# Long convolution with a gated feed-forward layer: the second transposition of each row tile moves from TensorE to the DMA queue

## What is computed

```python
xp = (X @ Wp + bp).reshape(B, T, STAGES + 1, D)
f = (pos @ Wf + bf).reshape(T, STAGES, D)
y = xp[:, :, 0, :]
for i in range(STAGES):
    y = causal_convolution(y, f[:, i]) * xp[:, :, i + 1, :]
x = layernorm(X + y)
h = silu(x @ wg.T) * (x @ wu.T)       # wg, wu: 768 x 256, integers / 127
out = layernorm(x + h @ wd.T)         # wd: 256 x 768
```

## Time and profile before

| | |
|---|---|
| median of three runs | 779.73 us (778.16 to 781.01) |
| the profiled execution's own time | 778.79 us |
| its span in the trace | 777.0 us |
| TensorE busy | 745.4 us, 96% of the span |
| VectorE, ScalarE, GpSimd busy | 552.3, 489.0, 419.3 us |

### The profile page before, as it was taken

One profiled execution on the slowest core, in us unless ns is written; L12 is line 12 of the kernel. 1 busy time (PEld: TensorE's weight loads), 2 busy tenths in 40 slices (PEclk: granted clock), 3 DMA queues, 4 the chain that ended last, 5 costly groups with the idle time before them and its releaser, 6 DMA issues.

```text
span 777.0 us, 16267 instructions
## 1 busy us (share of the span) xinstructions
PE 745.4 (96%) x6068; PEld 563.3 (72%) x6068; DVE 552.3 (71%) x1092; ACT 489.0 (63%) x976; POOL 419.3 (54%) x483
## 2 busy tenths in 40 slices
PE   6999999999999999999999998889999999999996
PEld 5888877888788888888888886546565666556663
DVE  4787777777788888888888887655565566565544
ACT  3444544443487788878886664455677766677744
POOL 3445544554243444534444345686777777777553
PEclk9999999999999999999999999999999999999998
DMA  8659757999899999999899997111111231110101
GB/s 290 220 181 328 247 192 261 313 318 313 302 282 246 253 260 263 252 260 258 248 261 272 286 321 218 45 55 55 55 54 55 63 99 58 55 55 28 54 30 54
DMA packets 161997, 144.97 MB, mean 187 GB/s; under 512 B 4096, under 2 KB 145408, under 8 KB 161664
## 3 DMA queue, kind: packets, MB, share of 16 engines
q1 hardware_dynamic: 160064, 138.50, 58.8%
q10 hardware_dynamic: 1856, 5.44, 2.1%
HBM read 109.58 MB, written 34.34 MB: 185 GB/s over the span
## 4 chain that ended last, share of the span: by engine, by line
PE 90%; DVE 3%; DMA 2%; POOL 2%; issue 1%; ACT 1%; POOLq 0%; DVEq 0%; ACTq 0%
PE bank L374 22%; PE bank L446 20%; PE bank L428 19%; PE bank L467 10%; PE bank L387 8%; PE bank L408 3%; PE bank L409 3%; PE bank L410 3%; PE bank L438 2%; DMA toep<-filter_rows 2%; DVE prod L791 2%; POOL x L233 1%; PE bank L505 1%; PE bank L483 1%; DMA xt<-in_XT 1%
## 5 line engine op out<-in xcount | busy, mean ns | idle before, releaser
L978 POOL TENSOR_TENSOR y<-y,gate 128x512 f32<-128x512 f32 (+1 forms) x108 | 124.3, 1155 | 174.5 <-DVE y L815 162.4
L374 PE MATMUL bank<-wps,xs 128*128 128x512 f32 x768 | 182.5, 397 | 9.2 <-DVE wps L749 6.9
L428 PE MATMUL bank<-prod,ei 128*128 128x256 f32 x720 | 186.2, 381 | 0.0
L374 PEld LDWEIGHTS bank<-wps,xs 128*128 128x128 f32 x768 | 144.8, 190 | 40.9 <-POOL xs L1005 10.0
L791 DVE TENSOR_TENSOR prod<-bank,wfx 128x512 f32<-128x512 f32 x180 | 124.2, 690 | 41.1 <-PE bank L387 41.1
L1005 POOL TENSOR_TENSOR xs<-xt,xs 128x256 fp32r<-128x256 f32 x128 | 92.9, 742 | 105.2 <-ACT xs L578 105.0
L446 PE MATMUL bank<-xh,wq 128*128 128x512 f16 x384 | 145.7, 380 | 2.0 <-DVE hf L856 1.6
L446 PE MATMUL bank<-xl,wq 128*128 128x512 f16 x384 | 145.8, 380 | 0.0
L997 POOL TENSOR_TENSOR hl<-hf,hh 128x512 f16<-128x512 f32 x95 | 109.2, 1158 | 54.2 <-ACT hh L635 54.0
L428 PEld LDWEIGHTS bank<-prod,ei 128*128 128x128 f32 x720 | 123.1, 191 | 11.3
L856 DVE SCALAR_TENSOR_TENSOR hf<-bank,sg 128x512 f32<-128x512 f32 x96 | 64.3, 685 | 93.9 <-ACT sg L631 47.5
(11 more groups left out here) (78 smaller groups left out, 1255.3 us busy)
## 6 DMA issues: line engine op xcount, KB each, us to landing
toep<-filter_rows SPq DMA_DIRECT2D x43, 1024.0 KB, 8.0
gate<-gates SPq DMA_DIRECT2D x48, 512.0 KB, 4.4
xt<-in_XT SPq DMA_DIRECT2D x31, 512.0 KB, 5.7
gates<-st SPq DMA_DIRECT2D x24, 512.0 KB, 3.7
gates<-toep SPq DMA_DIRECT2D x24, 512.0 KB, 4.2
xr<-in_X SPq DMA_DIRECT2D x16, 512.0 KB, 5.0
out_x<-oo SPq DMA_DIRECT2D x15, 512.0 KB, 3.3
toep<-filter_rows SPq DMA_DIRECT2D x10, 512.0 KB, 6.8
```

Source lines behind the costliest of these rows:

```text
L374: mm = pe.matmul(b_proj[n % PBK][:, :], xs[:, n % XSS, hx, k, :], wps[:, hw, k, p * 512:(p + 1) * 512], start=(k == 0 and q == 0), stop=(k ...
L428: mm = pe.matmul(b_out[m % 2][:, half * W:(half + 1) * W], ei[:, h, e0 * P:(e0 + 1) * P], prod[:, n % 3, h, :], start=(h == 0), stop=(h == 1))
L978: nc.gpsimd.tensor_tensor(y[:, u % NG, a:a + count, :], y[:, u % NG, a:a + count, :], gate[:, a:a + count, :], ALU.mult).then_inc(gated, 1)
```

## The change

Only tile 0 is still transposed by TensorE. From tile 1 on, ScalarE and VectorE split the rows as they stand (one instruction of 128x1024 elements each, `split_x` and `low_x`, into the new tiles xhn and xln), and SyncE issues two transposing DMAs (fp16, 256 KB each) into xh and xl (`turn`). `turn(k + 2)` stands in SyncE's loop between the wait for the end of TensorE's block k and `store(k)`. `split_x(k + 2)` stands at the end of ScalarE's block k, ahead of `norm2`. `norm1(k + 2)` moves to after m = 4 and m = 5. The down product stands after m = 2, and on VectorE `product(k, 2)` ahead of `sum2`. The table `cm` is halved: two products of 256 columns per stage in place of four, and four VectorE instructions on 64 partitions in place of two on 128. The last readout of the convolution comes ahead of the first up product, and one small Silu is put early into ScalarE's last unit.

```diff
@@ -97,16 +98,18 @@
-            xh = sb("xh", [P, 2, KT, NTOK], F16, ffn)
-            xl = sb("xl", [P, 2, KT, NTOK], F16, ffn)
+            xh = sb("xh", [P, 2, NB, KT, P], F16, ffn)
+            xl = sb("xl", [P, 2, NB, KT, P], F16, ffn)
+            xhn = sb("xhn", [P, 2, NB, D], F16, ffn)
+            xln = sb("xln", [P, 2, NB, D], F16, ffn)
-        cb = sb("cb", [P, 4])
-        cm = sb("cm", [P, 2, 2, P])
+        cb = sb("cb", [P, 2])
+        cm = sb("cm", [P, 2, P])
@@ -333,6 +343,12 @@
...
 
+                def turn(k):
+                    for src, dst, ready, done in ((xhn, xh, xhn_ready, xh_in), (xln, xl, xln_ready, xl_in)):
+                        sp.wait_ge(ready, k)
+                        sp.dma_start_transpose(dst[:, k % 2].rearrange("p b t n -> p (b t) n"),
+                                               src[:, k % 2].rearrange("p b c -> p (b c)")).then_inc(done[k % 2], 16)
+
                 def store(k):
@@ -349,10 +365,14 @@
...
                     load_rows(k + 2)
+                turn(1)
                 for k in range(NA):
...
                         load_rows(k + 5)
+                    if k + 2 < NA:
+                        sp.wait_ge(u_done, (k + 1) * HM)
+                        turn(k + 2)
                     if k < NA - 1:
@@ -429,21 +449,23 @@
...
 
-                def transposes(k):
-                    pe.wait_ge(x1n_ready, k * NB + NB)
-                    if k >= 1:
-                        pe.wait_ge(xl_ready, k * KT)
+                def transposes():
+                    pe.wait_ge(x1n_ready, NB)
                     for t in range(KT):
                         for b in range(NB):
-                            mm = pe.transpose(b_t[t][:, b * P:(b + 1) * P], x1n[:, k % 3, b, t * P:(t + 1) * P], ident[:])
+                            mm = pe.transpose(b_t[t][:, b * P:(b + 1) * P], x1n[:, 0, b, t * P:(t + 1) * P], ident[:])
                         mm.then_inc(tr_done, 1)
...
                 def ffn_up(k, m, wt, dst):
-                    pe.wait_ge(xh_ready, k * KT + KT)
-                    pe.wait_ge(xl_ready, k * KT + KT)
+                    if k == 0:
+                        pe.wait_ge(xh_ready, KT)
+                        pe.wait_ge(xl_ready, KT)
+                    else:
+                        pe.wait_ge(xh_in[k % 2], turns(k))
+                        pe.wait_ge(xl_in[k % 2], turns(k))
                     for t in range(KT):
                         for v in (xh, xl):
-                            mm = pe.matmul(dst[:, :], wt[:, t, m * P:(m + 1) * P], v[:, k % 2, t, :],
+                            mm = pe.matmul(dst[:, :], wt[:, t, m * P:(m + 1) * P], v[:, k % 2, :, t, :],
                                            start=(t == 0 and v is xh), stop=(t == KT - 1 and v is xl))
@@ -500,15 +522,14 @@
...
                         pe.wait_ge(f_tmp, 6)
-                        for r in range(2):
-                            for h in range(2):
-                                mm = pe.matmul(c_bank[i][:, r * D:(r + 1) * D], cm[:, h, r, :], wf[:, h, i * D:(i + 1) * D],
-                                               start=(h == 0), stop=(h == 1))
+                        for h in range(2):
+                            mm = pe.matmul(c_bank[i][:, 0:D], cm[:, h, :], wf[:, h, i * D:(i + 1) * D],
+                                           start=(h == 0), stop=(h == 1))
                         mm.then_inc(c_done, 1)
...
                 pe.wait_ge(s_tab, 64)
-                pe.wait_ge(wfx_ready, 2 * NS)
+                pe.wait_ge(wfx_ready, 4 * NS)
                 for n in range(NT):
@@ -534,11 +555,13 @@
...
                             pe.wait_ge(toep_out, NU * NQ)
-                            transposes(0)
+                            transposes()
                         if u < NU and k < NE:
...
                             readout(u, k - 1)
+                        if k == NA - 1 and u == NU - 1:
+                            readout(u, NA - 1)
                         if k == 14 and u == NU - 1:
@@ -548,16 +571,14 @@
...
                             up_part(0, 1)
-                        if k == 0 and u >= 1:
+                        if k == 0 and 1 <= u < NU:
                             readout(u - 1, NA - 1)
...
                             up_part(k, m)
-                        if m == 1:
-                            if k + 1 < NA:
-                                transposes(k + 1)
+                        if m == 2:
                             if k >= 1:
@@ -619,10 +640,17 @@
...
 
+                def split_first():
+                    act.wait_ge(tr_done, KT)
+                    for t in range(KT):
+                        nc.scalar.activation(xh[:, 0, :, t, :], b_t[t][:, :].rearrange("p (b n) -> p b n", b=NB), ACT.Copy,
+                                             scale=XS).then_inc(xh_ready, 1)
+
                 def split_x(k):
-                    act.wait_ge(tr_done, k * KT + KT)
-                    for t in range(KT):
-                        nc.scalar.activation(xh[:, k % 2, t, :], b_t[t][:, :], ACT.Copy, scale=XS).then_inc(xh_ready, 1)
+                    act.wait_ge(x1n_ready, k * NB + NB)
+                    if k >= 3:
+                        act.wait_ge(xh_in[k % 2], turns(k - 2))
+                    nc.scalar.activation(xhn[:, k % 2], x1n[:, k % 3], ACT.Copy, scale=XS).then_inc(xhn_ready, 1)
 
@@ -709,30 +737,33 @@
...
                         if u == NU - 1:
+                            if k == 1:
+                                nc.scalar.activation(warm[:], ones[:, 0:1], ACT.Silu)
                             if 1 <= k <= 6:
...
                             if k == 10:
-                                split_x(0)
+                                split_first()
                             if k == 13:
                                 norm1(1, range(NB))
+                                split_x(1)
                 for k in range(NA):
...
                     high_h(k, 0)
-                    if k + 1 < NA:
-                        split_x(k + 1)
                     high_h(k, 1)
-                    silu(k, 2)
-                    if k + 2 < NA and k >= 1:
-                        act.wait_ge(zz_ready, k * 2 + 1)
-                    for m in range(3, HM):
+                    for m in range(2, HM):
                         silu(k, m)
-                        high_h(k, m - 1)
-                        if m < HM - 1 and k + 2 < NA:
-                            norm1(k + 2, range(2 * m - 6, 2 * m - 4))
+                        if m >= 3:
+                            high_h(k, m - 1)
+                        if m >= 4 and k + 2 < NA:
+                            if m == 4 and k >= 1:
+                                act.wait_ge(zz_ready, k * 2 + 1)
+                            norm1(k + 2, range(2 * m - 8, 2 * m - 6))
                     high_h(k, HM - 1)
+                    if k + 2 < NA:
+                        split_x(k + 2)
                     if k >= 1:
@@ -798,13 +829,14 @@
...
                     for r in range(2):
-                        sign = r == 1 and turned(i)
-                        nc.vector.scalar_tensor_tensor(
-                            out=wfx[:, i * NG:(i + 1) * NG, r, :],
-                            in0=bfr[:, i * D:(i + 1) * D].rearrange("p (g c) -> p g c", c=CG),
-                            scalar=cb[:, 2 * turned(i) + r:2 * turned(i) + r + 1],
-                            in1=c_bank[i][:, r * D:(r + 1) * D].rearrange("p (g c) -> p g c", c=CG),
-                            op0=ALU.mult, op1=ALU.subtract if sign else ALU.add).then_inc(wfx_ready, 1)
+                        rows = slice(r * NF, (r + 1) * NF)
+                        for half in (slice(0, NF), slice(NF, P)):
+                            nc.vector.scalar_tensor_tensor(
+                                out=wfx[half, i * NG:(i + 1) * NG, r, :],
+                                in0=bfr[rows, i * D:(i + 1) * D].rearrange("p (g c) -> p g c", c=CG),
+                                scalar=cb[rows, turned(i):turned(i) + 1],
+                                in1=c_bank[i][rows, 0:D].rearrange("p (g c) -> p g c", c=CG), op0=ALU.mult,
+                                op1=ALU.subtract if r == 1 and turned(i) else ALU.add).then_inc(wfx_ready, 1)
 
@@ -841,12 +873,19 @@
...
 
+                def low_first():
+                    for t in range(KT):
+                        dve.wait_ge(xh_ready, t + 1)
+                        nc.vector.scalar_tensor_tensor(
+                            out=xl[:, 0, :, t, :], in0=b_t[t][:, :].rearrange("p (b n) -> p b n", b=NB), scalar=XS,
+                            in1=xh[:, 0, :, t, :], op0=ALU.mult, op1=ALU.subtract).then_inc(xl_ready, 1)
+
                 def low_x(k):
-                    for t in range(KT):
-                        dve.wait_ge(xh_ready, k * KT + t + 1)
-                        nc.vector.scalar_tensor_tensor(out=xl[:, k % 2, t, :], in0=b_t[t][:, :], scalar=XS,
```

(28 more changed lines are left out.)

## The result

| | before | after |
|---|---|---|
| median, us | 780.37 (778.16 to 782.4, 4 runs) | 803.78 (801.72 to 805.24, 4 runs) |
| profiled span, us | 777.0 | 801.3 |

The ratio is 1.030, with an interval of 1.028 to 1.032: the change costs 3%. The forecast was 793.0 in a range of 783 to 813, a rise of 13.3 us. The measured rise is 23.4 us: the wait that was forecast is there, and 10 us come on top of the sum.

A forecast was written before the change was run, and what follows sets the result against it. TensorE, which never waits in the last third, bounds the kernel, with ScalarE next. Transposes -13.05, stalls +28.95 and coefficients -2.6 make +13.3 us on the median of 779.73: 793.0 us, range 783 to 813.

The forecast's parts named there:

- The wait: TensorE ahead of m = 2 waits for ScalarE's late silu, 2.10 us a block, making blocks of 17.7 us.
- 27.3 and 0.48: Forecast TensorE stalls: 13 times 2.10 ahead of m = 2 in blocks 2 to 14, and 0.48 us in block 15.
- The clock adds nothing: TensorE's granted clock was expected to hold through waits of 2.1 us, costed at nothing; a fall would raise the time.
- case (A): Forecast case, 68%: ScalarE's queue is the new wait for TensorE, 785 to 800 us.
- The coefficient products: Three TensorE groups of 1.73 us become 0.87: 2.6 us less; VectorE's added 2.5 us costed at nothing.
- Tile 1's transposes: Two DMAs of 4.0 us, one after the other, land late, so TensorE waits 3.92 us ahead of block 1.
- quick transposes: Transposing DMAs at 2.2 us: tile 1's wait falls under 1 us, and the sum is 2.0 us less.
- The timetable: Layout of all five queues in the block stage: TensorE stalls sum to 32.1 us after, 3.15 before.
- a stall of 0.38: TensorE's forecast wait in block 0 of the kernel after, 0.38 us.
- B: Rival, 22%: transposing DMAs are slow, tiles arrive late in every block; 812.5 us at 8.0 each, 844 at 10.
- C: Rival, 7%: faster, as ScalarE clears its block end sooner; each 0.4 us shorter per block takes about 5.3 us.
- D: Rival, 3%: no difference, ScalarE's run at the end of the block being exactly 1.0 us shorter.

The follow-up runs named there:

- Experiments 1 and 3: Both on the changed kernel: 1 put the down product back after m = 1, 777.06 us; 3 moved norm2 into the down product, 768.12 us.
- experiment 2: Changed kernel with eight unused filler matmuls between m = 1 and m = 2 of blocks 2 to 14: 796.87 us, ratio 1.022.
- experiment 6: Kernel before with the coefficient products alone halved: 779.18 us, ratio 0.998.
- Experiment 8: Changed kernel with one more transposing DMA per tile, into a scratch tile, between the two needed: 802.79 us, ratio 1.029.
- experiment 7: Kernel before with the last readout of the convolution alone put ahead of the first up product: 777.8 us, ratio 0.997.

## Why the prediction was right, and what its sum missed

**The wait: right.** Place, releaser and price were as written: 2.10 us a block, blocks of 17.7; measured 17.81 where the clock holds, of which 15.60 are matmuls. The list of waits has 28.1 us that end with the silu, where the prediction had 27.3 and 0.48 of them. Experiments 1 and 3 remove the wait from either side, by giving ScalarE the down product to catch up or by taking norm2 out of its way.

**The clock: wrong.** "The clock adds nothing: TensorE stood still for 1.6 us with the granted clock at 1.00, and 2.1 is little more" is the step that failed. The time is not in the pause alone. It came to 8.4 us in five blocks of the profiled execution, and experiment 2 gives 0.8% back by filling the pauses. One harmless pause of 1.6 us was no evidence for thirteen pauses of 2.1. The same prediction said that the time would go up and not down if the clock did fall, but gave that no price; the nearest one was at hand: 7.1 us of matmuls follow each wait, and at half speed throughout they would take 7.1 us more. It came to 1.67 in five blocks of thirteen. Why it falls after five of them and not after the others no run shows.

**The number: in part luck.** The forecast case (A) had 785 to 800 us, and 803.78 is above it. The range reached to 813 because it held room for slow transposes, which did not come; the clock, costed at nothing, used that room. Without its 8.4 us the time would be an estimated 795.4, inside case A.

**The coefficient products: mis-sized.** -2.6 was -1.2 alone (experiment 6). "I cost it at nothing" looked at VectorE; what comes up in the chain is ScalarE's squares.

**Tile 1's transposes: mis-sized.** The 3.92 us ahead of block 1 aren't there, and the sum is 2.0 smaller for it, as the prediction said for quick transposes (the wait for the silu in block 1 comes up in its place, 1.05 us). No wait of the stage names a DMA; the first pair was issued at 508.54 and 509.93 us, a moment later than forecast for the high part, but the low part went out 1.4 us behind it, not after it had landed. I had laid the pair out one after the other at 4.0 us each. Single landings are near that (4.3 and 5.5 us at the median), but they overlap: block 1, which needs both, starts at 514.30, so the pair took at most 5.8 us from the first issue, and not 8.0. Experiment 8 brings out what was spared: the low part issued at 512.56 costs 1.5 us.

**The sum.** I take the stage from the first gate product to the first matmul of the last down product: 500.72 to 764.12 us before, 500.60 to 788.37 after, so 263.4 and 287.8, 24.4 longer. The timetable had 15.9; the clock took 8.4, and without it the stage is 16.0 longer. Within that, -2.0 for tile 1 and 13 x 0.1 for the blocks leave 0.8. The rows have a term of about that size in block 0, where the timetable had a stall of 0.38 (TensorE in order of time; VectorE's low parts, with minimum, median and maximum in ns):

```profile
511.56 0.39 PE L468 MATMUL bank<-xh,wq 128*128 128x512 f16 x1 [1.47 <-DVE hf L895]
```

```profile
L887 DVE SCALAR_TENSOR_TENSOR xln<-x1n,xhn x15: 1212/1215/2775, 506.4 to 759.2; 128x1024 f16<-128x1024 f32 x15
```

The low part of tile 1, at 506.4 us, is the one of 2.77 us; the prediction priced it at 1.22. It runs beside GpSimd's add (from 505.23 us, 2.88 long), and behind it on VectorE stand the statistics and the product that TensorE waits for. So the 1.6 us that experiment 7 removes did not leave the changed kernel. That the add is what slowed the low part is read from the times alone.

Ahead of the stage the kernel after is 0.1 us early and not 2.6: in this pair of executions nothing of the coefficient products was left, while the medians of experiment 6 give them 1.2. So 13.3 + 8.4 + 2.5 + 0.1 = 24.3, the growth of the span.

**The rivals.** B (slow transposes) fell in experiment 8. On the two entries of the Trainium skill that disagreed: by "DMA: Bandwidth & Descriptors", section on latency and other measured facts, 256 KB would be near the low end; by "VectorE: DVE Perf Modes", section on the three transpose paths, eight blocks in a row would be an estimated 10.5 us. The trace of the changed kernel has, for all 30 together:

```profile
DMA to landing us min/median/max: 3.0/5.3/7.2
```

The longest is under the second estimate, though a store and a load of rows are often in front. The shortest, 3.0, is above the low end of 2.2. So the trace lies between the two, and the estimate of 10.5 is too long in every case; a bandwidth by itself was not measured. C (ScalarE faster than its pitches) did not happen: the rows of norm2 took 1.97 for four, as before. A small slip: the shares that the range leaves out, half of B with C and D, sum to 21% and not 20.

## What to carry to other kernels

When work leaves a queue that never waits, look for who had been late behind it: the removed 0.87 us and the moved 5.24 us were the cover of ScalarE's last four rows. Lay out the run of the next busiest queue from the trace's start-to-start times, between the point where it is released and the point where it is needed; it gave the block to 0.1 us, and the same layout named the repair, which is to put the late work where that queue idles. Give a pause of a busy TensorE a second price, matmuls behind it at half clock; in this kernel it was 1.67 us after five of thirteen pauses.

## What was not expected

- **Pauses of 2 us can cost more than themselves, and not every time.** Of thirteen equal waits of 2 us, five were followed by a stretch at the lower clock, and so it was again in the kernel of experiment 8; with the fillers in them none was.
- **GpSimd's low parts got slower, and once VectorE's.** The 95 instructions on hl take 1293 ns on average, with 1158 before. VectorE's new low part reads and writes SBUF alone, where the one it replaces read PSUM; two hl next to it took 3.12 us, where a pair takes 2.28. The rows are of GpSimd and VectorE in the changed kernel:

```profile
643.62 2.28 POOL L1036 TENSOR_TENSOR hl<-hf,hh 128x512 f16<-128x512 f32 x2
649.27 3.12 POOL L1036 TENSOR_TENSOR hl<-hf,hh 128x512 f16<-128x512 f32 x2 [3.37 <-ACT hh L663]
```

```profile
649.05 1.22 DVE L887 SCALAR_TENSOR_TENSOR xln<-x1n,xhn 128x1024 f16<-128x1024 f32 x1
```

  In blocks 2 to 14 it cost nothing, since GpSimd waits for ScalarE there; in block 0 the slow low part of VectorE stands in front of TensorE's wait of 1.47 us. That the one slows the other is read from the times alone; no run separated them.
- **A transposing DMA occupies SyncE's queue** for 1.2 to 4.2 us at its issue, where the plain ones in the rows above took 0.38 and 0.51. No wait of TensorE in the changed kernel names what stood behind it.
